# A transformer stack on one core: first queries, identity products, a mask and one output product are moved or rewritten

## The reference

```python
x = _layernorm(x + _L0_attn_ref(x, ...))      # state-space scan, 8 heads of 64
x = _layernorm(x + _L0_xattn_ref(x, ctx, ...)) # cross-attention, 16 heads of 64
x = _layernorm(x + _L0_ffn_ref(x, ...))       # mixture of 8 experts, top 2, hidden 512
x = _layernorm(x + _L1_attn_ref(x, ...))      # latent self-attention, causal, 16 heads
x = _layernorm(x + _L1_xattn_ref(x, ctx, ...)) # cross-attention, 8 heads of 128
x = _layernorm(x + _L1_ffn_ref(x, ...))       # linear + 8 gated low-rank products
```

## Time and profile before

| | us |
|---|---|
| median of 3 runs | 1011.96 |
| lowest and highest | 1010.72, 1013.11 |
| the profiled execution | 1011.95 |
| its span (first to last instruction) | 1010.1 |

### The profile page before, as it was taken

How to read it: one execution, slowest core, us unless ns; L and a number is a source line. 1 busy time by engine, 2 the same in 40 slices (tenths; PEclk the granted TensorE clock), 3 DMA queues, 4 the chain that set the end, 5 groups by cost and what they waited for, 6 DMA issues and landing times. The chain is left out here.

```text
span 1010.1 us, 16932 instructions
## 1 busy us (share of the span) xinstructions
PE 965.1 (96%) x6432; PEld 747.1 (74%) x6432; DVE 575.1 (57%) x1307; ACT 408.1 (40%) x1069; POOL 154.3 (15%) x151
## 2 busy tenths in 40 slices
PE   9899799999999999989999999989989999999985
PEld 4678687878778777768999998656666777777663
DVE  3887546555555556566756555358644444555544
ACT  3556434343343333335454544357633232332221
POOL 0323610110110100004443432300010000000000
PEclk9999899999999999989999999989999999999998
DMA  4500100000000000019311000710000000000000
GB/s 158 202 1 1 53 16 1 17 17 1 16 2 1 1 2 1 1 39 290 119 42 49 35 1 21 173 21 2 3 18 17 16 16 16 16 1 25 6 6 18
DMA packets 26824, 36.32 MB, mean 36 GB/s; under 512 B 3648, under 2 KB 22160, under 8 KB 26752
## 3 DMA queue, kind: packets, MB, share of 16 engines
q1 hardware_dynamic: 26752, 35.35, 12.0%
HBM read 30.75 MB, written 2.75 MB: 33 GB/s over the span
## 5 line engine op out<-in xcount | busy, mean ns | idle before, releaser
L1128 ACT ACTIVATE x_prob<-bank,x_negmax 112x375 f32<-112x375 f32 x128 | 72.2, 569 | 144.0 <-DVE x_negmax L1038 144.0
L1847 DVE TENSOR_TENSOR moe_h_low<-moe_sq,moe_h_high 128x512 fp32r<-128x512 f32 (+1 forms) x64 | 54.4, 872 | 53.6 <-ACT moe_h_high L1947 40.9
L1924 POOL TENSOR_TENSOR moe_sq<-moe_r 128x512 f32<-128x512 f32 (+1 forms) x64 | 64.2, 1006 | 105.7 <-ACT moe_r L1956 83.9
L1038 DVE TENSOR_REDUCE x_negmax<-bank 112x1 f32<-112x375 f32 x128 | 64.1, 543 | 9.6 <-PE bank L926 7.3
L1956 ACT ACTIVATE moe_r<-bank 128x512 f32<-128x512 f32 (+1 forms) x64 | 34.9, 546 | 75.7 <-PE bank L101 68.7
L101 PE MATMUL bank<-moe_w_low,moe_h_high 128*128 128x256 f32 x224 | 63.4, 283 | 0.0
L101 PE MATMUL bank<-moe_w_high,moe_h_low 128*128 128x256 f32 x224 | 63.3, 283 | 0.0
L101 PE MATMUL bank<-moe_w_high,moe_h_high 128*128 128x256 f32 x224 | 63.3, 283 | 0.0
L1043 DVE COPY x_prob_t<-bank 125x336 f32<-125x336 f32 x128 | 58.4, 497 | 2.8 <-PE bank L935 1.4
L926 PE MATMUL bank<-x_kt,x_qt 64*112 64x375 f32 x256 | 58.3, 521 | 1.2 <-DVE x_kt L1030 0.7
L935 PEld LDWEIGHTS bank<-const,x_prob 112*125 112x125 f32 x384 | 49.8, 188 | 6.6 <-issue 3.8
(11 more groups left out here) (370 smaller groups left out, 2252.2 us busy)
## 6 DMA issues: line engine op xcount, KB each, us to landing
moe_w<-in_L_ffn_W SPq DMA_DIRECT2D x15, 512.0 KB, 5.0
ctx_t<-in_ctx_t SPq DMA_DIRECT2D x8, 376.0 KB, 4.3
x_ctx_t<-in_ctx_t SPq DMA_DIRECT2D x8, 376.0 KB, 3.2
wk<-in_L_xattn_Wk SPq DMA_DIRECT2D x2, 1024.0 KB, 5.3
wv<-in_L_xattn_Wv SPq DMA_DIRECT2D x2, 1024.0 KB, 8.4
wq<-in_L_xattn_Wq SPq DMA_DIRECT2D x2, 1024.0 KB, 10.5
wo<-in_L_xattn_Wo SPq DMA_DIRECT2D x2, 1024.0 KB, 12.0
xt<-in_xt SPq DMA_DIRECT2D x1, 896.0 KB, 4.7
```

The source lines that it names most:

```text
L1038: dve.tensor_reduce(negmax[:, g:g + 1], S_BANK(u, e)[0:T, 0:S], AX_X, ALU.max, negate=True).then_inc(max_ready, 1)
L1128: act.activation(PROB(u, e)[:, :], S_BANK(u, e)[0:T, 0:S], ACT.Exp, bias=negmax[:, g:g + 1], accum_out=total[:, g:g + 1]).then_inc(p_ready, 1)
L1847: dve.tensor_tensor(h_low[half][:, m, 0:size], sq[m % 2][:, 0:size], h_high[half][:, m, 0:size].bitcast(F32), ALU.subtract).then_inc(low_d ...
L1924: pool.tensor_tensor(sq[m % 2][:, 0:size], r[m % 2][:, 0:size], r[m % 2][:, 0:size], ALU.mult).then_inc(sq_done, 1)
```

## The change

Five edits, each in its own stage:

1. The four first "q" jobs of `cross_attention` become `first_queries(0)` to `(3)`, issued by TensorE in the last rounds of `state_space`, into banks 2, 3, 5, 6. They are emptied at the start of the next block, two by VectorE and two by ScalarE.
2. `stream`: products of a 128x128 identity by itself, whose result nobody reads: 11 before the last NT of `cross_attention`, 9 after the projections of the latent stage's first block, 8 before the last NT of the program.
3. `hide_later(1, range(2))` moves from the end of the latent round r = -1 to behind the folds at r = 0.
4. The OUT product of the wide stage is done from rounded operands in three products for each one. `collect` makes the high parts on ScalarE (three copies) and then the low parts on VectorE (three subtractions); the weights `w_b` are split by both engines in the first three pairs of item 0.
5. At item 0, pair 0 of the wide stage the EARLY job stands ahead of the next scores and not behind them.

```diff
@@ state_space, its last rounds on TensorE
+                def first_queries(a):
+                    pe.wait_ge(core.xw_loaded, 80)
+                    pe.wait_ge(nt_copied, 2)
+                    pe.wait_ge(mix_ready, B)
...
+                    for m in range(2):
+                        at = slice((2 * a + m) * 128, (2 * a + m + 1) * 128)
+                        accumulate(pe, core.query_bank[a][:, m * 2 * T:(m + 1) * 2 * T], [
+                            (core.wq[:, c, at], core.xt[:, c, 0:2 * T]) for c in range(KD)])
...
+                    if r == B:
+                        first_queries(0)
                     if there(r - 1):
                         turn_y(r - 1)
                     if there(r + 1):
                         log_decay(r + 1)
+                    if r == B:
+                        first_queries(1)
                     if there(r - 1):
                         out_projection(r - 1)
+                    if r == B + 1:
+                        first_queries(2)
+                        first_queries(3)
                     if there(r - 2):
                         turn_state(r - 2)
@@ cross_attention: fronts, scores, VectorE and ScalarE ahead of their rounds
             if i < 0:
-                return [("q", (0, a)) for a in range(4)]
+                return []
...
+                        if i == 0:
+                            pe.wait_ge(first_act, 2)
+                            pe.wait_ge(first_dve, 2)
...
+                for a in (1, 3):
+                    empty_queries(0, a, core.query_bank[a], copy).then_inc(first_dve, 1)
...
                 act.preload_act_table_set(EXP_LN)
+                for a in (0, 2):
+                    empty_queries(0, a, core.query_bank[a], copy).then_inc(first_act, 1)
@@ identity products
+def stream(pe, out, ident, count):
+    for k in range(count):
+        pe.matmul(out[:, 0:128], ident, ident, start=True, stop=True)
...
+                        if i == B:
+                            stream(pe, S_BANK(0, 0), ident, 11)
                         pe.wait_ge(normed_ready, i)
...
+                    stream(pe, bank[B_LAT], core.c(128, C_ID, 128), 9)
...
+                    if job_ == (NT, B - 1):
+                        stream(pe, S_BANK[0], ident, 8)
@@ wide_cross_attention: second output product
-        ot = sb("ot", [128, 3, J, T])
+        ot_high, ot_low = sbr("ot_high", [128, 3, J, T]), sbr("ot_low", [128, 3, J, T])
+        w_b_high, w_b_low = sbr("w_b_high", [128, M, D]), sbr("w_b_low", [128, M, D])
...
                         last = accumulate(pe, out[0:T, 0:D], [
-                            (ot[:, e, j, :], w_b[:, 2 * j + e if e < 2 else G + j, :]) for e in range(3) for j in range(J)])
+                            pair for e in range(3) for j in range(J) for pair in split_products(
+                                ot_high[:, e, j, :], ot_low[:, e, j, :], w_b_high[:, at(e, j), :], w_b_low[:, at(e, j), :])])
...
-                        pe.wait_ge(ot_act, 2 * i + 2)
-                        pe.wait_ge(ot_dve, 2 * i + 2)
+                        pe.wait_ge(ot_split, 2 * i + 2)
...
-                    dve.wait_ge(pv_done, 2 * i + half + 1)
...
-                    dve.tensor_copy(ot[:, 1, ...], U_BANK[1][:, cols]...).then_inc(ot_dve, 1)
+                    dve.wait_ge(ot_rounded, 2 * i + half + 1)
+                    for e in range(3):
+                        last = dve.tensor_tensor(ot_low[:, e, heads, :], U_BANK[e][:, cols]...,
+                                                 ot_high[:, e, heads, :].bitcast(F32), ALU.subtract)
+                    last.then_inc(ot_split, 1)
...
-                    act.copy(ot[:, 0, ...], U_BANK[0][:, cols]...)
-                    act.copy(ot[:, 2, ...], U_BANK[2][:, cols]...).then_inc(ot_act, 1)
+                    for e in range(3):
+                        last = act.copy(ot_high[:, e, heads, :], U_BANK[e][:, cols]...)
+                    last.then_inc(ot_rounded, 1)
...
+                        if i == 0 and u < 3:
+                            split_weights(u)
@@ latent_attention, second block, TensorE
                         if r == 0:
                             prepare_all(AHEAD, FILL)
+                            hide_later(1, range(2))
...
-                        if there(r + 2):
+                        if r >= 0 and there(r + 2):
                             hide_later(r + 2, range(2))
```

More of the change, by code:

```diff
@@ L156, in __init__ @@
         self.bank = [ctx.enter_context(nc.psum_tensor(f"bank{k}", [128, 512], F32)) for k in range(8)]
+        self.query_bank = [self.bank[k] for k in (2, 3, 5, 6)]
         self.loaded = ctx.enter_context(nc.semaphore("const_loaded"))
@@ L1345, in _ @@
                     for u in range(J):
+                        if i == 0 and u == 0:
+                            for job_ in jobs(i, u, EARLY):
+                                job(job_)
                         if u + 1 < J:
@@ L1349, in _ @@
                             scores(i + 1, 0)
-                        for job_ in jobs(i, u, EARLY):
-                            job(job_)
+                        if i > 0 or u > 0:
+                            for job_ in jobs(i, u, EARLY):
+                                job(job_)
                         turn(i, u)
@@ L1591, in _ @@
                             collect(i - 1, 1)
+                        if i == 0 and u < 3:
+                            round_weights(u)
                         if u == 1 and i > 3:
```

36 lines of the change are left out of this document (24 added, 12 removed).

## The result

The changed kernel takes 1000.46 us in the median of five executions (994.54 to 1001.15), the kernel before 1011.96 (1008.16 to 1013.54): ratio 0.9887, 95% interval 0.9855 to 0.9918. The ratios given are not quotients of the medians (1000.10 over 1012.50 would be 0.9878), so the two can differ. The changed kernel is faster by 11.5 us, where 18.9 were forecast; 1000.46 lies outside the range.

A forecast was written before the change was run, and what follows sets the result against it. TensorE was taken as the bound, busy 965.1 of 1010.1 us. The terms −4.2 − 2.6 − 1.5 − 6.1 − 5.3 + 0.8 sum to −18.9, from 1011.95 to 993.0; own range 989.5 to 996, wider range 988 to 999.5.

The forecast's parts named there:

- First queries: Cross-attention's front: four query jobs issued earlier fill TensorE's waits, so the first key product comes sooner; 4.2 us faster.
- Identity products: Before the mixture and at the latent stage's start: identity products keep the clock up; 2.6 and 1.5 us faster.
- Cost 0: The eleven identity products before the mixture take at most 2.4 us, ending before the norm, so cost nothing.
- The mask: Latent stage: masks behind the folds save TensorE's idling and keep the folds at full clock; 6.1 us faster.
- The output product: Wide stage: three-pass OUT product shortens each job, less the price on VectorE; 5.3 us faster in sum.
- −7.4 of product: Wide stage: 36 records in 4.3 us instead of 24 in 5.36, 1.06 less per job over seven jobs.
- +2.1 of price: Wide stage, items 6 and 7 and the end: later collection on VectorE costs 0.7, 0.6, 0.6 and 0.2 us.
- The early job, 0: Wide stage, item 0: moving the EARLY job ahead of the second scores changes nothing, 0 us.
- The tail: Program's end: eight identity products push the end by 1.3 us, a higher clock saves 0.5; 0.8 us slower.
- Rival 1: Whole kernel: the clock falls elsewhere, the mixture's 2.6 stays lost and the keys run slow; 997.6 us, chance 0.17.

The follow-up runs named there:

- the fourth trace: The changed kernel with nothing altered, profiled a fourth time, on a third chip: 999.50 us.
- mask_back: The changed kernel with the first two masks of the latent stage ahead of the folds again: 1000.20 us, ratio 0.9890 to the kernel before.
- float_product: The changed kernel with the wide stage's output product in float32 again and the old copies: 1001.88 us, ratio 0.9891 to the kernel before.
- early_alone: The kernel before with only the early job of item 0 moved ahead of the next scores: 1015.20 us, ratio 1.0036 to the kernel before.
- early_back: The changed kernel with the early job of item 0 behind the next scores again: 995.29 us, ratio 0.9847 to the kernel before.
- no_identity_no_early: The changed kernel without the identity products and with the early job behind the scores again: 1000.19 us, ratio 0.9901 to the kernel before.
- the last experiment: The changed kernel with early job back and last weighing ahead of the transposes (993.24 us), without all identity products: 995.10; without the last eight alone: 994.32.
- changed's second: The second profiled trace of the changed kernel, with nothing altered: 1000.49 us.

## Why the prediction was wrong

By its steps, for the execution of 1000.49 (its whole difference, −11.5, is the sum of the table's rows).

- **First queries, −4.2:** the key product stands 6.5 earlier. Some 0.6 is given back within the cross-attention (from the first key product to its last OUT product 315.9 us, before 315.3): −5.9, and 5.8 in the medians. The four jobs take 1.6 each and filled more of the gaps (116.78: two jobs in 3.20 us). Right mechanism, term 1.7 too small.
- **Identity products, −2.6 and −1.5:** −2.6 and −1.4 in the rows of the table. "Cost 0" was wrong at the first place:

```profile
441.75 2.72 PE L122 MATMUL bank<-const 128*128 128x128 f32 x22 [0.59 <-DVE x_res L1096]
444.30 0.36 PE L1014 MATMUL bank<-const,x_normed 112*128 112x112 f32 x2
```

  They start 0.59 us into the wait and take 2.55 to the transposes, 3.14 in all where the wait was 2.58, so the transposes are 0.56 late. Against that, the higher clock starts the mixture 0.8 sooner (before, 325.46 in the table; 324.62 in the fourth trace, where the fall comes later). Together −2.9. At the second place up to 0.4 more of waiting in the traces of changed leaves −1.0 to −1.4. Over all twenty traces, the start of the mixture was low in nine of nine without these products and in two of eleven with them; the start of the latent stage in six of nine and in none of eleven. So the mechanism was right. On the medians they are −4.9 in the kernel without the early job, clear of the intervals; −1.9 with the weighing moved, and +4.6 in changed, both inside them.
- **The mask, −6.1:** −5.9. Against mask_back's one trace 4.3, since there the identity products keep most of the folds at full clock.
- **The output product, −5.3:** −4.65 over six jobs (the job takes 0.94 less; 0.8 to 0.9 of it is left at five, 0.45 at the sixth), and then +0.86 in the last item even where the clock stays up, with nothing won behind it. So −3.8 at full clock; I had −7.4 of product and +2.1 of price, and the product was over-sized: the job was 4.42, not 4.3, so seven are 6.6 (the starts are 0.120 apart, as forecast). Against this, not in the sum at all: behind the longer waits of the last item (3.09 and 2.05) the clock falls in three of four traces of changed, in that of 1000.49 for another 3.0 to the eighth OUT and 1.7 behind it, 1.5 of it in the last OUT's own records. These 4.7 are the larger part of what the forecast missed. That the waits are not needed for a fall there, float_product and early_alone show.
- **The early job, 0:** at full clock it is 0 (mask_back: 45.76). But it puts TensorE's wait behind the transposes, 1.49 us, and there the clock fell in every trace of changed: +1.6. Alone, in the kernel before, its median is 3.1 slower, of which its trace shows 1.6 at this place. "Changes nothing" was the worst of my steps: I had looked at whether the job ends something sooner, and not at where it moves the idling.
- **The tail, +0.8:** 0 in the 994.54 trace, as it ends at 18.70 against 18.73. Against kernels with the new product and no such products the tail gains: early_back takes 18.39 where no_identity_no_early takes 19.27, 18.38 against 19.49 in the last experiment. Here the sign was wrong.
- **The end of the latent stage**, which no edit touches, was low in two of four traces of changed (+1.7) and in none of four before. Over all traces it was low in eight of the fourteen of changed and its variants and in none of the six built on the kernel before. That was not a step of mine.

Added up for the execution of 1000.49: −5.9 (queries), −2.9 and −1.0 (identity), −5.9 (mask), −3.8 (product), 0 (tail) give −19.5, close to the −18.9 of the forecast, and the falls in three new places give back 4.7, 1.6 and 1.7, together 8.0. That the sum came so near is in part luck: queries came out larger and the product smaller by about the same. The step that failed is the assumption under the sum, that a stretch at 0.5 can be taken away and none comes, and with it the early job's term of 0. Rival 1, at 0.17 and 997.6, had this as its title, "the clock falls elsewhere"; but the two places that it priced, the mixture's start and the keys, were up in three of four and in four of four traces of changed. The places that fell were others, and two of them hold waits that the edits made or lengthened. By the mean clocks, the kernel before spends some 35 us at the low level in an execution (mean of twenty), changed 22 (mean of eleven). From the profiled 36 I had taken four of five stretches away, 27, which leaves 9.

**Open.** Why the end of the latent stage falls in changed and not before: no edit is near, and in an execution the low stretches shift against the program, so that a stage which only starts at another time may be hit. And why removing the early job brings 4.8 where 1.6 stand in its place: in early_back's one trace the time to the eighth OUT is 16.98 and the end 18.39, 1.3 and 2.0 less than in changed's second; with the 1.6 that makes 4.9. That fits, but was not isolated, and the same two traces differ at other places, too (7.24 and 5.62 at the mixture, 72.32 and 74.00 to the first wide scores). And why the clock falls in the last item behind the old waits in two traces of six.

## What to carry to other kernels

Where the clock falls in gaps, price an edit twice: at full clock, from the starts on TensorE, and by where it puts TensorE's idling. Look at several executions with their mean clock before believing one trace; here the first was 6 us from the median. Shortening the wait (the weighing ahead of the transposes) took 1.6 us off the last item at full clock; filling it with products that compute nothing took none off, and its one trace has a fall behind it (medians 993.24 and 996.44 on one chip, with intervals that overlap). Where executions come in groups 5 us apart, a median of five can jump from one group to the other: compare the means and intervals as well.

## What the runs showed of the hardware

Executions of one program differ by up to 9 us (992.41 to 1001.19, on one chip) with no instruction changed, and the mean clock goes with it: a line through the eleven executions of changed gives 0.43 us of span for each microsecond at the low level. In the traces of changed each low stretch before the end is 3.4 or 6.8 us long, also behind a wait of only 1.49 us (738.7 to 742.0 behind the wait that ended at 737.23; 736.6 to 740.0 behind 735.98), and where it starts against the wait differs between executions. Waits of 1.90 us (kernel before, item 0 of the wide stage) had no fall behind them in four traces. The weight split, 1.22 us for 1024 columns, had no price that a trace shows: with it, in early_back, it is 45.77 us to the first OUT, as before.
